# A graph network on one core: runs of wide matmuls whose result nobody reads, and 50 rounds instead of 62 gathered ahead

## What is computed

```
h = relu(layernorm(x))
out_deg, in_deg = how often each node is a sender, a receiver (at least 1)
x = x + segment_sum((h * out_deg**-0.5)[src], dst) * in_deg**-0.5
n = LN(mlp(relu(layernorm(x))));  e = LN(mlp(edge_attr))
for s in range(2):
    e = e + LN(mlp([e, n[src], n[dst]]))
    n = n + LN(mlp([n, segment_sum(e, dst)]))
x = x + mlp(n)
```

## Time and profile before

| What | Value |
|---|---|
| median of three runs | 12,188.99 us (12,187.57 to 12,226.75) |
| profiled execution, its own time | 12,209.74 us |
| its span in the trace | 12,207.6 us |
| granted PE clock, mean over the span | 0.706 of full speed |
| `edge_lists` ends, first gather of `first_layer` | 880.8 us |
| first gather of the first edge step | 4308.7 us |
| first gather of the second edge step | 8259.7 us |

### The profile page before, as it was taken

How to read it: one execution, slowest core, us unless ns; L and a number is a source line. 1 busy time by engine, 2 the same in 40 slices (tenths; PEclk the granted TensorE clock), 3 DMA queues, 4 the chain that set the end, 5 groups by cost and what they waited for, 6 DMA issues and landing times. The chain is left out here.

```text
span 12207.6 us, 205656 instructions
## 1 busy us (share of the span) xinstructions
PE 9418.6 (77%) x61843; PEld 7006.0 (57%) x61843; DVE 5449.0 (45%) x11082; ACT 5439.2 (45%) x8544; POOL 9088.1 (74%) x9512
## 2 busy tenths in 40 slices
PE   4778999999899867777777777776677767777776
PEld 4657777887788745554555555554444444444444
DVE  8825555555555534444444444443333333333333
ACT  1004555555555544444444444444444444444444
POOL 7877777777777567777777777777777777777776
PEclk8755555555655677777777777777777777777777
DMA  2122222222222233333344444443333333333333
GB/s 83 40 54 39 42 41 42 41 44 48 47 46 47 49 87 94 96 95 96 95 98 103 104 104 103 104 97 71 69 70 68 70 68 71 72 72 72 72 72 60
DMA packets 1307481, 868.68 MB, mean 71 GB/s; under 512 B 826377, under 2 KB 986906, under 8 KB 1306317
## 3 DMA queue, kind: packets, MB, share of 16 engines
q1 hardware_dynamic: 907938, 582.70, 17.7%
q0 software_dynamic: 303584, 232.40, 13.0%
q10 hardware_dynamic: 95408, 47.86, 1.5%
HBM read 630.95 MB, written 247.05 MB: 72 GB/s over the span
## 5 line engine op out<-in xcount | busy, mean ns | idle before, releaser
L1898 POOL DMA_INDIRECT edge_blk_g<-sender_part,idx_all x6272 | 5918.5, 944 | 2058.3 <-issue 1910.9
L144 POOL DMA_INDIRECT gather_ring<-sender_x,idx_all x2752 | 2600.3, 945 | 868.6 <-issue 829.6
L1954 PE MATMUL edge_blk_hps<-ident,edge_blk_g 128*128 128x128 f32 x6256 | 1235.0, 359 | 2021.3 <-DMA edge_blk_g<-sender_part,idx_all 2020.6
L1954 PEld LDWEIGHTS edge_blk_hps<-ident,edge_blk_g 128*128 128x128 f32 x6256 | 1055.2, 254 | 2772.7 <-DMA edge_blk_g<-sender_part,idx_all 2747.5
L1970 ACT ACT_TABLE_LOAD x1564 | 2006.6, 1283 | 58.9 <-ACTq L1069 31.5
L2042 DVE SCALAR_TENSOR_TENSOR agg<-edge_blk_aggps,vecs,agg 64x64 f32 x1564 | 442.3, 283 | 3091.3 <-PE edge_blk_aggps L1914 2930.5
L1984 ACT ACTIVATE edge_blk_h<-edge_blk_hps,vecs 128x512 f32<-128x512 f32 x782 | 537.4, 687 | 2852.7 <-PE edge_blk_hps L1954 2840.7
L1949 PE MATMUL edge_blk_hps<-edge_blk_oha,edge_blk_win 128*128 128x512 f32 x1564 | 1154.4, 828 | 27.9 <-DMA edge_blk_win<-receiver_part 27.9
L1603 ACT ACT_TABLE_LOAD x782 | 1003.3, 1283 | 368.1 <-PEq L87 354.3
L1937 PEld LDWEIGHTS edge_blk_yps<-w_edge_blk,edge_blk_h 64*128 64x128 f32 x12512 | 1012.9, 242 | 246.0 <-issue 245.9
L1937 PE MATMUL edge_blk_yps<-w_edge_blk,edge_blk_h 64*128 64x64 f32 x12512 | 1135.7, 336 | 1.2 <-issue 1.2
(11 more groups left out here) (294 smaller groups left out, 11871.3 us busy)
## 6 DMA issues: line engine op xcount, KB each, us to landing
edge_blk_e<-edge_state SPq DMA_DIRECT2D x782, 256.0 KB
edge_blk_g<-sender_part,idx_all POOLq DMA_INDIRECT x6272
edge_state<-fl_e SPq DMA_DIRECT2D x391, 256.0 KB
edge_blk_dlb<-local_dst SPq DMA_DIRECT2D x1564, 64.0 KB
edge_state<-edge_blk_new SPq DMA_DIRECT2D x391, 256.0 KB
gather_ring<-sender_x,idx_all POOLq DMA_INDIRECT x2752
edge_blk_win<-receiver_part SPq DMA_DIRECT2D x1564, 16.0 KB
fl_attr<-attr_slots SPq DMA_DIRECT2D x391, 32.0 KB
```

Source lines behind the costliest of these rows:

```text
L144: pool.indirect_dma_start(out=gr[:, n % RING, j, :], out_offset=None, in_=table, in_offset=bass.IndirectOffsetOnAxis(ap=idx_all[:, 8 * n + ...
L1898: pool.indirect_dma_start(out=g[n % QUAD][:, i, 64 * c:64 * c + 64], out_offset=None, in_=ps_d, in_offset=bass.IndirectOffsetOnAxis(ap=idx ...
L1954: ins = nc.tensor.matmul(h_ps[n.half][:, P * i:P * i + P], g[n.b][:, i, :], ident[:, :], start=False, stop=i == TILES - 1)
```

## The change

There are three edits.

- **AHEAD** goes from 62 to 50. POOL gathers 12 rounds less in `edge_lists` and 12 more in `first_layer`.
- **Before the lookup** PE gets 30 matmuls of 128 rows by 512 columns. Their operand `busy` is a new tile of ones, which DVE sets at the beginning (so `zero_ok` counts one more), and they write a PSUM tile that `look(1)` overwrites.
- **In the first layer** a helper `stream(k)` issues k matmuls of 96 rows by 512 columns from operands that are there already, into a PSUM tile of the node work that nobody reads at that time. 16 stand before the first round, and 8 between `encode` and `turn_in` of the rounds 0 to 5 and of every fourth round of the loop.

```diff
-AHEAD = 62
+AHEAD = 50
...
+        busy = sb("busy", [P, CHUNK], BF16)
...
                 v.memset(one_f[:, :], 1.0).then_inc(zero_ok, 1)
+                v.memset(busy[:, :], 1.0).then_inc(zero_ok, 1)
...
+                for _ in range(30):
+                    nc.tensor.matmul(z_ps[1][:, 1, :], busy[:, 0:P], busy[:, :], start=True, stop=True)
                 pe.wait_ge(parts_ok, 1)
                 look(0)
...
                     second(n.back(2))
                     encode(n.back(1))
+                    if i is None and (n.b == QUAD - 1 if not isinstance(n.m, int) else n.n < 6):
+                        stream(8)
                     turn_in(n)
...
+                def stream(k):
+
+                    for _ in range(k):
+                        nc.tensor.matmul(n_ps[:, :], one_bf[:, :], b1_parts[:, :], start=True, stop=True)
...
                 pe.wait_ge(prepared, 1)
+                stream(16)
                 last = rounds_and_nodes(pe, body, count_sb, 2)
```

More of the change, by code:

```diff
@@ L834, in body @@
                     else:
-                        act.wait_ge(zero_ok, 4)
+                        act.wait_ge(zero_ok, 5)
                     nc.scalar.activation(srow_f[:, :], srow[:, :], ACT.Copy)
@@ L860, in _ @@
                 v.memset(one_f[:, :], 1.0).then_inc(zero_ok, 1)
+                v.memset(busy[:, :], 1.0).then_inc(zero_ok, 1)
                 v.memset(deg[:, :], 0.0).then_inc(zero_ok, 1)
                 v.memset(zero_col[:, :], 0.0).then_inc(zero_ok, 1)
-                dve.wait_ge(zero_ok, 4)
+                dve.wait_ge(zero_ok, 5)
                 dve.wait_ge(base_in, 32)
@@ L899, in _ @@
                 v.tensor_copy(deg[0:NHI, :], d_ps[0:NHI, 0:P]).then_inc(zero_ok, 1)
-                dve.wait_ge(zero_ok, 5)
+                dve.wait_ge(zero_ok, 6)
                 v.tensor_scalar(rs[:, :], deg[:, :], 1.0, None, ALU.max).then_inc(most_ok, 1)
@@ L960, in _ @@
                                     ident[0:MAX_BLOCKS, 0:MAX_BLOCKS]).then_inc(base_turned, 1)
-                pe.wait_ge(zero_ok, 4)
+                pe.wait_ge(zero_ok, 5)
                 nc.tensor.matmul(d_ps[0:NHI, 0:P], zeros[:, 0:NHI], zeros[:, :], start=True, stop=False, skip_group_check=True)
```

## The result

| | before | after |
|---|---|---|
| median of 12 executions | 12,194.2 us (12,169.8 to 12,226.8) | 12,244.2 us (12,176.0 to 12,302.3) |
| ratio | 1 | 1.0033 (95% interval 1.0020 to 1.0046) |
| profiled execution, its span | 12,207.6 us | 12,275.4 us |
| `edge_lists` ends, first gather of `first_layer` | 880.8 us | 807.8 us |
| first gather of the first edge step | 4308.7 us | 4372.9 us |

The change made the kernel about 40 to 50 us slower, where +119 was foretold. The sign was right and the size was not.

The account below looks back on a forecast made before the run. PE's round with DVE and ACT was taken to bound the first layer, POOL's gathers the edge steps. AHEAD −60.6, the 30 −2.6, runs +182.3 − 3.6 − 3.4 + 6.9 gave +119: 12,308 us, range 12,200 to 12,335.

Parts of the forecast that it names:

- the sum: Whole kernel: −60.6 − 2.6 + 182.3 − 3.6 − 3.4 + 6.9 = +119 us.
- What bounds: First layer: PE, DVE and ACT's round ends last; PE ends at about 4428, POOL at 4233.
- AHEAD 50: `edge_lists`: POOL finishes before the lookup, everything behind starts earlier and ring waits go; −60.6 us.
- the part then ends with the later of this and the lookup: End of `edge_lists`: POOL's gathers end at 749.1, the lookup at 809.4, so the lookup sets it.
- The 30 matmuls: Ahead of the lookup, where PE waits 6.53 us: first 12 lookup matmuls at full clock, −2.6 us.
- The steps that follow are the same in the new kernel: Lookup: after a fast start the clock falls as before, so the rest of the lookup stays unchanged.
- The runs: First layer, between `encode` and `turn_in`: 424 matmuls at 0.43 us, nothing hiding them, +182.3 us before small savings.
- the runs pay for themselves in part: First layer rival: each run raises the clock and shortens one round by 1.97 us, 104 back; 12,204 us, chance 0.09.
- its two objections: Against runs paying in part: a run is 8, not 12; savings must fall on `second` and `encode`, not PE's wait.
- the clock stays high: Rival, lookup and first layer at full clock: 12,098 us, chance 0.11; first layer only, 12,158 us, chance 0.04.
- The trace does not bear it out for what the profile calls busy: Lookup: 240 us of PE busy all the time stayed at clock 0.50, against sustained activity releasing the throttle.
- Its price for the tail: End of first layer: 45 us from POOL's last gather to the edge step if POOL bounds it.

Follow-up runs that it names:

- the runs alone: Against the kernel before: only the 16 matmuls and 53 runs of 8 in the first layer, AHEAD 62, no 30; 12,300.7 us, before beside it 12,210.4.
- the second profile of before: The kernel before, unchanged, profiled once more; it took 12,227 us (beside it 12,159).
- The last kernel: Against before: AHEAD 55, 8 matmuls of 128 rows behind `turn` in loop rounds ahead of node work, no 30, no `stream` runs; 12,116.4 us, before 12,225.4.

## Why the prediction was right and wrong

The profiled span grew by 67.8 us against the +119 of the sum. Stage by stage, from the starts of `turn_in` (the eighth and the 200th round as marks):

| Stage | foretold | measured |
|---|---|---|
| start of the layer, first `turn_in` | −56.3 (−60.6 − 2.6 + 6.9) | −66.0 (890.6 to 824.6) |
| first 8 rounds, 6 runs | +17.2 (6 × 3.44 − 3.4) | +5.0 (64.8 to 69.8) |
| next 192 rounds, 47 runs | +158.1 (47 × 3.44 − 3.6) | +111.6 (1643.8 to 1755.4) |
| 190 rounds with node work | 0 | +14.2 (1643.0 to 1657.2) |
| from there to the end | 0 | +2.9 |

- **What bounds.** Right. POOL issued its 342 rounds from 807.8 to 4226.6 without a wait (4233 foretold), PE was 80 us later at its last `turn_in` (4307.0), and the first gather of the edge step came 64.2 us later, 28.9 by POOL's later last gather and 35.2 by the longer hole.
- **AHEAD 50.** The mechanism was right, and it was worth 9 us more than the step "the part then ends with the later of this and the lookup", to which I added the barrier's 10.7 us. The barrier took 10.74 when POOL arrived last and 1.77 when DVE did. At this barrier the trace before had only the first case.
- **The 30 matmuls.** The mechanism was right: the first 12 of `look` ran at the full clock, and the lookup then stayed at 0.50 ("The steps that follow are the same in the new kernel"). That they gained 2.6 us is not shown. The lookup ended 3.4 us earlier, but 1.9 of this was there before they began (the histogram ended at 523.6 instead of 525.5). From its first to its last `look` it took 266.4 us with them, 267.8 and 267.7 in the two profiles of before, and 265.9 in the runs alone, which lack them.
- **The runs.** This is the step that failed: "nothing hides them: 424 × 0.43 = +182.3, less what they save where the clock is high at that moment". That they stand on the loop was right (12.05 us a round, and no overlap). I credited only the matmuls themselves with the clock as it was before, 0.52. But the clock answers to them, and other rounds grow shorter too. The foretold 175.3 for both stages became 116.6, or 103.6 against the second profile of before. So 59 us more came back than I had credited (72 by the second profile). In the loop, the 47 rounds with a run took 11.55 us on average, 3.0 more than the 8.56 of before instead of 3.44, and the 144 others 8.36, 0.2 less; that is 21 and 29 us back, where 3.6 was credited. 12 of the 59 came in the opening rounds, where the clock over the first eight went from 0.50 to 0.65:

```profile
890.60:955.40 64.80, 51.88 (x295) 44.42 (x296) 35.26 (x103) 29.43 (x46) 40.11 (x43) 0.50 0.18 26
```

```profile
824.60:894.50 69.90, 56.89 (x336) 42.38 (x335) 35.50 (x104) 29.44 (x46) 52.84 (x57) 0.65 0.17 26
```

- **The rival "the runs pay for themselves in part"** named this mechanism at 12,204 with 1.97 us back per run. About 1.1 us per run came back beyond my credit (59 / 53), in the profiled execution. It deserved more than 0.09, and its two objections were both too strong: a high clock does follow runs of 8 now and then, and in the pair shown above the saving does fall on `second` and `encode`.
- **The node rounds.** Nothing changed there, and the same 190 rounds took 1648.8 in the second profile of before and 1619.6 with the runs alone. So their +14.2 lies within what single executions differ by.
- **The rest** up to the medians is the choice of execution: the profiled one of after lies 33 us above its median, that of before 16, so 67.8 becomes 50. The executions of after spread over 126 us (before 57), and the slowest has a mean clock of 0.712, the fastest two 0.723 and 0.724. That the return differs from one execution to the next fits this, but no trace of a fast one was taken.
- **The first rival, "the clock stays high",** ends on the other side, and its mechanism exists: with full tiles of ones and a dose in each round it happened, and the end was set by POOL as worked out there. What it needs is not what the change brings. "The trace does not bear it out for what the profile calls busy" was a sound reading of rows with 98-row matmuls. The TensorE page of the Trainium skill ("TensorE: Matmul & The Clock Gate", Part 1) has sustained matmul activity release the throttle. The last kernel agrees with it, at 0.88 over 1700 us. The lookup, which the profile shows busy in 240 of 240 us at 0.50 in both kernels, does not.
- **Its price for the tail**, 45 us, was 35.24 once POOL set the end. AHEAD 50 without runs was foretold at −31. My estimate from these rows is 807.8 + 342 × 10.0 + 35 = 4263 against 4308.7, −46, which was not measured.

## What to carry to other kernels

Matmuls that nobody reads have two effects: their length where they stand, and what the granted clock then makes of the rounds behind them. Put them where PE waits anyway. 424 of 96 rows ahead of a transpose that the other engines wait for cost 182 us by the sum and gave back 66 to 79. 1528 full tiles of ones in PE's waits were all but free. Before that, ask what the next bound is: with PE at full clock the layer ran into POOL. Up to round 200 the rounds had gained 300 us (1643.8 − 1343.9) and the earlier start 67, and 94 arrived.

When a barrier's cost is read from a trace, see which engine arrived last: another one arriving last may pay another price.

## What the runs showed of the hardware that I had not expected

- The granted clock differed with what the wide matmuls held, at the same length and place: 0.50 without runs, 0.52 with 96 rows of which three are not zero, 0.55 with 128 rows of ones. With full tiles of ones in each round it was 0.88 over 1700 us. Rows and values were not told apart.
- The barrier behind `edge_lists` took 10.74 us when POOL came last, straight from issuing gathers, and 1.23 to 1.77 when DVE did. Why was not tried.
